# Two roundings of squares moved later in ScalarE's order, in a fused cross-attention and feed-forward kernel

## The chip, the cores and the metric

The kernel runs on one core of one Trainium2 chip. The metric is the device time of one execution in microseconds (us). A core has five engines that run beside each other and meet at semaphores: TensorE (PE; its weight loads are listed apart as PEld), VectorE (DVE), ScalarE (ACT), GpSimd (POOL) and SyncE (SP), which issues the DMAs. Each engine works through its own instructions in the order in which the program lists them: an instruction that waits holds all that stand behind it on its engine.

## What is computed

```python
x = x + tanh(g_xattn) * xattn(layernorm(x), ctx)
x = x + tanh(g_ffn)   * ffn(layernorm(x))
# xattn: 16 heads of 32, softmax(Q K^T / sqrt(32)) V, then Wo; 154 context rows per batch
# ffn, with x_prev the row before:
xr = mu_r * x + (1 - mu_r) * x_prev
xk = mu_k * x + (1 - mu_k) * x_prev
out = sigmoid(xr @ W_r.T) * (square(relu(xk @ W_k.T)) @ W_v.T)
```

x is (4, 2048, 512) in float32, all weights are 512 x 512. The product with W_v needs the squares of all 512 columns of relu(k).

## The kernel before, in words

The 8192 rows are cut into 16 blocks of 512 tokens. Every float32 product is made of three products of parts: each operand is split into an upper part (HI, rounded by a copy on ScalarE) and a lower part (LO, the source minus the upper part, a subtraction on VectorE or GpSimd), and TensorE multiplies HI by HI, HI by LO and LO by HI. A product of 512 x 512 by 128 columns is thus 12 matmuls of 128x128 by 512 columns.

Each engine has a function `step(i, ffn, pre)`, which is called for block 0 with ffn False, for blocks 1 to 14 in a hardware loop with both True, and for block 15 with pre False. A step works on the attention of block i and, with ffn True, on the feed-forward part of block i - 1; with pre True also on the first norm and the queries of block i + 1. The order of the work in a step is written out by hand, per engine.

The attention of a block goes through four groups g of four heads. For a group, TensorE makes scores of four banks (`head_scores`, L1187) and of the 26 tail rows of the context (`tail_scores`, L1202), ScalarE takes two exponentials of each of the five banks (`exps(i, g, n)`, n = 0 to 4, L656: one into `pq` as float16 at L662, one in place at L663), VectorE subtracts (`p_low`, L890), and TensorE multiplies with the values (`values`, L1209, waits for all five `p_low` of the group). VectorE then divides by the sum of the exponentials (`attend(i, g)`, L894: transposed, reciprocal, transposed, multiplied, each waiting for the one before, into `attn32`), ScalarE rounds that (`attn_high`, L675) and GpSimd makes its lower part (`attn_low`, L488).

The squares of relu(k) come in four chunks c of 128 columns, through two buffers in turn, `k2[c % 2]`, which are two slots of `place`:

- relu: chunks 0 and 1 on ScalarE (`k_relu`, L651), 2 and 3 on VectorE (`k_relu`, L911). VectorE's waits at L913 until the lower part of chunk c - 2, which reads the same buffer, is made: `k2_lo >= i*C + c - 1`.
- square: `k2_square(i, c)` on GpSimd (L480), in place.
- upper part: `k2_high(i, c)` on ScalarE (L647, recorded as L568, a helper), into `buf1`.
- lower part: `k2_low(i, c)` on GpSimd (L484), which waits for the upper part.

GpSimd's order (`k2_parts`, L500) is square 0, low 0, square 1, low 1, square 2, low 2, square 3, low 3. Behind it in the step stand the small operations of two norms (L449) and `attn_low(i, 0)`.

On VectorE, `k_relu(i-1, 2)` stands ahead of `p_low(i, 0, 0)` and `k_relu(i-1, 3)` behind `p_low(i, 0, 4)`; then come the moments of two tiles of the next block (`moments1`, L853), then `attend(i, 0)`, then `p_low(i, 1, 0)`.

TensorE's order from the first group's scores to the second group's values is: `head_scores(i, 0)`, `ffn_k(i-1, (3,))`, `tail_scores(i, 0)`, `ffn_r(i-1, 0)`, `values(i, 0)`, `head_scores(i, 1)`, `ffn_r(i-1, 1)` (waits for relu 3), `tail_scores(i, 1)` (waits for `p_low(i, 1, 0)`, L1203), `ffn_v(i-1, 0)` (waits for all four lower parts of the squares, L1301), `values(i, 1)`. These products are recorded at L1114, a helper; ffn_r's read WrT and ffn_v's read WvT.

Of the kernel before, what the change touches and what calls it, by code (L numbers as in the profile page):

```python
# [17 lines left out]
def flamingo_block(nc, x, ctx_columns, g_xattn, g_ffn, Wq, Wk, Wv, Wo, W_r, W_k, W_v, mu_r, mu_k, out):  # L18
# [30 lines left out]
    with ExitStack() as ctx:  # L49
# [516 lines left out]
        def _(act):  # L566
            def high(dst, src, done):
                nc.scalar.activation(dst, src, ACT.Copy).then_inc(done, 1)  # L568
# [19 lines left out]
            def kv_high(u):  # L588
                item, kind, n = KV[u]
                act.wait_ge(kv_done, u + 1)  # L590
                if item == 1 and kind == "k" and n >= 2:
                    act.wait_ge(later_stored[n - 2], 48)
                elif (item, kind, n) == (1, "v", 0):
                    act.wait_ge(v_stored, 32)
                    act.wait_ge(v_loaded, 16 * V_LOADS)
                if (item, kind, n) == (0, "v", 0):
                    act.wait_ge(mask_ready, 1)
                    nc.scalar.activation(kv_place(u, HI), kv_product(u), ACT.Copy, scale=mask[:, :]).then_inc(kv_hi, 1)
                else:
                    high(kv_place(u, HI), kv_product(u), kv_hi)  # L600
# [5 lines left out]
            def norm1(i, t):  # L606
                act.wait_ge(norm_ready[0], i * TT + t + 1)
                nc.scalar.activation(xa[:, t, :], xa[:, t, :], ACT.Identity, bias=nb[:, 0, t:t + 1],
                                     scale=rstd[:, 0, t:t + 1]).then_inc(xn1_ready, 1)
# [6 lines left out]
            def norm2(i, t, pre):  # L616
                if t >= 2:
                    act.wait_ge(x2_done, i * TT + t - 1)
                elif pre:
                    act.wait_ge(xT_done, (i + 1) * TT + t + 1)  # L620
                act.wait_ge(norm_ready[1], i * (TT - 1) + t + 1)
                nc.scalar.activation(xn2[t % 2], x1[:, t, :], ACT.Identity, bias=nb[:, 1, t:t + 1],  # L622
                                     scale=rstd[:, 1, t:t + 1]).then_inc(xn2_ready, 1)

            def xT_high(i, t):
                act.wait_ge(xT_done, i * TT + t + 1)
                later(act, q_done, i * G)
                high(xnT[:, HI, :, P * t:P * t + P], xT_bank[t][:, :].rearrange("p (c n) -> p c n", c=C), xT_hi)
# [14 lines left out]
            def q_split(i, g, loop):  # L643
                q_high(i, g, loop)
                q_copy(i, g, loop)

            def k2_high(i, c):  # L647
                act.wait_ge(k2_ready, i * C + c + 1)
                high(buf1[:, HI, c, :], k2[c % 2], k2_hi)

            def k_relu(i, c):  # L651
                act.wait_ge(k_done, i * C + c + 1)
                later(act, k2_lo, i * C)
                nc.scalar.activation(k2[c], K_BANK[c][:, :], ACT.Relu).then_inc(relu_ready[0], 1)  # L654

            def exps(i, g, n):  # L656

                m = 5 * g + n
                bank = score_bank[m]
                act.wait_ge(scores_done, i * SCORE_UNITS + m + 1)  # L660
                later(act, av_done, i * G + g)
                nc.scalar.activation(pq[:, n, HI, :], bank[:, :], ACT.Exp, scale=SCALE).then_inc(p_hi, 1)  # L662
                nc.scalar.activation(bank[:, :], bank[:, :], ACT.Exp, scale=SCALE).then_inc(p_full, 1)  # L663

            def tanh_r(i, t, bank=R_BANK):
                act.wait_ge(r_done, i * TT + t + 1)
                if t >= 2:
                    act.wait_ge(out_ready, i * TT + t - 1)
                else:

                    act.wait_ge(k2_lo, i * C + 1)
                    act.wait_ge(xr_mixed, i * C + 1)
                nc.scalar.activation(th[t % 2], bank[t][:, :], ACT.Tanh, scale=0.5).then_inc(th_ready, 1)

            def attn_high(i, g):  # L675
                act.wait_ge(attn32_ready, i * G + g + 1)
                high(buf3[:, HI, g, :], attn32, attn_hi)

            def x2_copy(i, t):
                act.wait_ge(x2_done, i * TT + t + 1)  # L680
                later(act, r_done, i * TT)
                dst, src = x2[:, :, 1 + P * t:1 + P * t + P], x2_bank[t][:, :].rearrange("p (c n) -> p c n", c=C)
                if t < TT - 1:
                    nc.scalar.activation(dst, src, ACT.Copy).then_inc(x2_ready, 1)
                else:

                    nc.scalar.activation(dst[:, 0:2, :], src[:, 0:2, :], ACT.Copy).then_inc(x2_half, 1)
                    nc.scalar.activation(dst[:, 2:4, :], src[:, 2:4, :], ACT.Copy).then_inc(x2_ready, 1)
# [5 lines left out]
            def xr_high(i, c):  # L694
                mix_high(i, buf2, c, xr_bank, xr_mixed, xr_hi)

            def xk_high(i, c):
                mix_high(i, buf3, c, xk_bank, xk_mixed, xk_hi)

            def mT_copy(i):  # L700
                act.wait_ge(mT_done, i + 1)
                high(mT[:, :], mT_bank[:, :], mT_ready)
# [20 lines left out]
            def fill_group(g):  # L723
                late = (units(5), units(6), ())[g]
                for u in late[:2]:
                    weight_high(u)
                kv_high(FIRST_LATER + 2 * g + 1)
                for u in late[2:]:
                    weight_high(u)

            def step(i, ffn, pre):
                if ffn:
                    k_relu(i - 1, 0)
                    k_relu(i - 1, 1)
                    xr_high(i - 1, 0)
                mT_copy(i)
                if ffn:
                    k2_high(i - 1, 0)
                    xr_high(i - 1, 1)
                    xr_high(i - 1, 2)  # L740
                exps(i, 0, 0)
                exps(i, 0, 1)
                if ffn:
                    xr_high(i - 1, 3)
                    k2_high(i - 1, 1)
                exps(i, 0, 2)
                exps(i, 0, 3)
                if not ffn:
                    kv_high(FIRST_LATER)
                exps(i, 0, 4)  # L750
                if ffn:
                    k2_high(i - 1, 2)
                    tanh_r(i - 1, 0)
                    k2_high(i - 1, 3)
                else:
                    fill_group(0)
                for g in range(1, G):
                    exps(i, g, 0)
                    exps(i, g, 1)
                    attn_high(i, g - 1)  # L760
                    if not ffn and g == 3:
                        kv_high(KV_UNITS - 1)
                    if pre and g == 3:
                        xT_high(i + 1, 0)
                    exps(i, g, 2)
                    exps(i, g, 3)
                    if not ffn and g < 3:
                        kv_high(FIRST_LATER + 2 * g)
                    exps(i, g, 4)
                    if ffn and (pre or g < G - 1):  # L770
                        tanh_r(i - 1, g)
                    elif not ffn and g < 3:
                        fill_group(g)
                    if pre:
                        for t in ((0, 1), (2, 3), ())[g - 1]:
                            norm1(i + 1, t)
                if pre:
                    for t in range(1, TT):
                        xT_high(i + 1, t)
                attn_high(i, G - 1)  # L780
                if not pre:
                    tanh_r(i - 1, TT - 1)
                if pre:
                    for g in range(G - 1):
                        q_split(i + 1, g, True)
                if not ffn:
                    for n in range(7):
                        act.wait_ge(later_stored[n], LATER_STORES[n])
                for t in range(TT):
                    if t < TT - 1:  # L790
                        norm2(i, t, pre)
                    x2_copy(i, t)
                if pre:
                    q_split(i + 1, 3, True)
                for c in range(C):
                    xk_high(i, c)

            step(0, False, True)
            with act.Fori(1, BLOCKS - 1) as i:
                step(i, True, True)  # L800
# [671 lines left out]
```

## Time and profile before

| | |
|---|---|
| time, median of 3 runs | 1404.73 us (1402.91 to 1406.04) |
| the profiled execution: its own time | 1408.19 us |
| the profiled execution: its span, first to last instruction | 1406.4 us |
| TensorE matmul busy | 1358.7 us, 97% of the span |
| VectorE busy | 1037.4 us, 74% |
| ScalarE busy | 777.4 us, 55% |
| GpSimd busy | 590.5 us, 42% |
| mean granted TensorE clock | 0.99 of full |

The loop blocks repeat to within a few hundredths of a microsecond, one every 83.0 us. In the timelines each line is a start in us from the span's start, a duration in us, the engine, the line of the kernel, the operation, what it writes and reads, how many were merged, and in brackets how long the engine had been idle before it and for whom. On ScalarE and VectorE the next instruction may start before the last one has fully ended, so steps in time are taken from start to start.

### The profile page before, as it was taken

The numbers are of one execution on the slowest core, as the hardware profiler recorded it, in microseconds if no ns is written. First come the engines' busy times: TensorE is split into PE (matmuls) and PEld (weight loads), VectorE is DVE, ScalarE is ACT, GpSimd is POOL, SyncE is SP. The second block draws the span as 40 slices with busy tenths as digits, with TensorE's granted clock in tenths as the row PEclk, the third lists the DMA queues.
The fourth block names the chain that finished last, engine by engine and source line by source line (L and its number), as shares of the span: only waits on it lengthen the run. The fifth ranks groups of instructions, "written<-read, shape, count | busy, mean of one in ns | idle before, by whom it ended". The sixth has DMA issues, their size and how long they took to land.

```text
span 1406.4 us, 27977 instructions
## 1 busy us (share of the span) xinstructions
PE 1358.7 (97%) x9436; PEld 992.8 (71%) x9436; DVE 1037.4 (74%) x1928; ACT 777.4 (55%) x1440; POOL 590.5 (42%) x786
## 2 busy tenths in 40 slices
PE   6889999999999999999999999999999999999988
PEld 5656676777767677676777767677776767777667
DVE  5867768687777868778786877868677686877652
ACT  5653746556374655737466473746637465573632
POOL 4333545343453534435353443525344352534333
PEclk8999999999999999999999999999999999999989
DMA  9421011212021121101212111121201112120101
GB/s 298 138 74 46 31 46 60 67 52 58 24 74 45 52 74 52 50 24 67 59 52 74 52 42 33 60 67 52 73 33 51 44 60 67 52 65 18 44 17 44
DMA packets 99179, 84.07 MB, mean 60 GB/s; under 512 B 49488, under 2 KB 64336, under 8 KB 99152
## 3 DMA queue, kind: packets, MB, share of 16 engines
q1 hardware_dynamic: 99152, 83.72, 19.5%
q8 instruction: 15, 0.25, 0.1%
q14 instruction: 12, 0.10, 0.0%
HBM read 57.75 MB, written 20.71 MB: 56 GB/s over the span
## 4 chain that ended last, share of the span: by engine, by line
PE 80%; DVE 8%; ACT 8%; issue 2%; DMA 1%; POOL 1%; SPq 0%; ACTq 0%; DVEq 0%
PE g_bank L1114 45%; PE g_bank L1274 7%; PE o_bank L1221 6%; PE s_bank L1195 4%; PE d_bank L1227 4%; ACT s_bank L663 3%; ACT pq L662 3%; PE s_bank L1171 3%; PE s_bank L1205 2%; DVE buf L815 2%; PE s_bank L1114 2%; PE d_bank L1120 2%; DVE o_bank L955 2%; PE o_bank L1120 1%; DVE d_bank L955 1%
## 5 line engine op out<-in xcount | busy, mean ns | idle before, releaser
L892 DVE TENSOR_TENSOR pq<-s_bank,pq 128x512 f16<-128x512 f32 x320 | 220.4, 689 | 68.9 <-ACT s_bank L663 68.4
L888 DVE TENSOR_REDUCE mm<-s_bank 128x3 f32<-128x462 f32 (+1 forms) x384 | 198.9, 578 | 96.1 <-PE s_bank L1171 96.1
L662 ACT ACTIVATE pq<-s_bank 128x512 f16<-128x512 f32 x320 | 192.2, 601 | 89.3 <-PE s_bank L1199 89.3
L1274 PE MATMUL g_bank<-buf,WkT 128*128 128x512 f32 x744 | 197.0, 412 | 8.6 <-DVE buf L815 6.9
L1114 PE MATMUL g_bank<-xnT,WqT 128*128 128x512 f32 x756 | 196.3, 406 | 0.0
L663 ACT ACTIVATE s_bank<-s_bank 128x512 f32<-128x512 f32 x320 | 194.6, 608 | 0.0
L1114 PE MATMUL g_bank<-WoT,buf 128*128 128x512 f32 x768 | 193.3, 401 | 0.0
L1114 PE MATMUL g_bank<-WrT,buf 128*128 128x512 f32 x744 | 184.2, 397 | 0.0
L490 POOL TENSOR_TENSOR buf<-place,buf 128x512 fp32r<-128x512 f32 x64 | 82.6, 1291 | 235.0 <-ACT buf L568 235.0
L1114 PE MATMUL g_bank<-WvT,buf 128*128 128x512 f32 x708 | 174.4, 395 | 0.0
L1274 PEld LDWEIGHTS g_bank<-buf,WkT 128*128 128x128 f32 x744 | 136.9, 192 | 51.7 <-DVE buf L815 13.8
L1114 PEld LDWEIGHTS g_bank<-WrT,buf 128*128 128x128 f32 x744 | 137.9, 188 | 40.2 <-issue 11.3
L1114 PEld LDWEIGHTS g_bank<-WoT,buf 128*128 128x128 f32 x768 | 140.8, 188 | 32.6
L1114 PEld LDWEIGHTS g_bank<-xnT,WqT 128*128 128x128 f32 x756 | 137.5, 190 | 35.6 <-DVE xnT L876 5.9
L1114 PEld LDWEIGHTS g_bank<-WvT,buf 128*128 128x128 f32 x708 | 130.7, 188 | 32.8 <-issue 5.8
L478 POOL TENSOR_TENSOR buf<-xa,buf 128x512 fp32r<-128x512 f32 x64 | 82.3, 1285 | 153.8 <-DVE d_bank L955 81.9
L568 ACT ACTIVATE buf<-place 128x512 fp32r<-128x512 f32 x128 | 81.0, 633 | 109.3 <-DVE place L909 74.8
L486 POOL TENSOR_TENSOR buf<-place,buf 128x512 fp32r<-128x512 f32 x64 | 83.2, 1300 | 94.0 <-ACT buf L568 94.0
L498 POOL TENSOR_TENSOR x<-place,x 128x512 f32<-128x512 f32 x48 | 61.7, 1286 | 123.1 <-DVE place L919 123.1
L622 ACT ACTIVATE xa<-x,nb,rstd 128x512 f32<-128x512 f32 x48 | 39.0, 813 | 105.2 <-POOL nb L460 104.9
L903 DVE STREAM_TRANSPOSE place<-d_bank 128x512 f32<-128x512 f32 x64 | 45.4, 709 | 62.2 <-PE d_bank L1227 59.1
L482 POOL TENSOR_TENSOR place<-place 128x512 f32<-128x512 f32 x64 | 78.2, 1221 | 25.6 <-ACT place L654 25.6
(145 smaller groups left out, 2087.9 us busy)
## 6 DMA issues: line engine op xcount, KB each, us to landing
xa<-in_x SPq DMA_DIRECT2D x64, 256.0 KB, 3.2
x<-in_x SPq DMA_DIRECT2D x64, 256.0 KB, 2.7
out<-x SPq DMA_DIRECT2D x48, 256.0 KB, 2.0
place<-x SPq DMA_DIRECT2D x16, 256.0 KB, 2.4
out<-place SPq DMA_DIRECT2D x16, 256.0 KB, 2.0
k_all<-k_scratch SPq DMA_DIRECT2D x15, 256.0 KB, 2.9
k_low<-k_scratch SPq DMA_DIRECT2D x15, 256.0 KB, 2.9
v_main<-v_scratch SPq DMA_DIRECT2D x15, 256.0 KB, 2.8
```

The costliest lines, as they stand in the source:

```text
L478: nc.gpsimd.tensor_tensor(buf4[:, LO, g, :], q32[g], buf4[:, HI, g, :].bitcast(F32), ALU.subtract).then_inc(q_lo, 1)
L482: nc.gpsimd.tensor_tensor(k2[c % 2], k2[c % 2], k2[c % 2], ALU.mult).then_inc(k2_ready, 1)
L486: nc.gpsimd.tensor_tensor(buf1[:, LO, c, :], k2[c % 2], buf1[:, HI, c, :].bitcast(F32), ALU.subtract).then_inc(k2_lo, 1)
L490: nc.gpsimd.tensor_tensor(buf3[:, LO, g, :], attn32, buf3[:, HI, g, :].bitcast(F32), ALU.subtract).then_inc(attn_lo, 1)
L568: nc.scalar.activation(dst, src, ACT.Copy).then_inc(done, 1)
L662: nc.scalar.activation(pq[:, n, HI, :], bank[:, :], ACT.Exp, scale=SCALE).then_inc(p_hi, 1)
L663: nc.scalar.activation(bank[:, :], bank[:, :], ACT.Exp, scale=SCALE).then_inc(p_full, 1)
L888: nc.vector.reduce_max(maxima, scores, AX.X).then_inc(reduced, 1)
L892: nc.vector.tensor_tensor(pq[:, n, LO, :], score_bank[5 * g + n][:, :], pq[:, n, HI, :], ALU.subtract).then_inc(p_lo, 1)
L1114: ins = nc.tensor.matmul(dst, stationary(s, c), moving(m, c), start=(c, n) == (0, 0), stop=(c, n) == (chunks - 1, len(PRODUCTS) - 1))
L1221: nc.tensor.matmul(o_bank[rows(j), :], v, pq[:, 4 if n else j, q, :], start=(n, k) == (0, 0), stop=(n, k) == (1, 2))
L1274: ins = nc.tensor.matmul(bank[c][:, :], WkT2[:, s, e, cols(c)], buf3[:, m, e, :], start=(e, n) == (0, 0), stop=(e, n) == (C - 1, len(PRODU ...
```

## The change

In ScalarE's step, with ffn True, three roundings of squares move. `k2_high(i-1, 1)` moves from ahead of `exps(i, 0, 2)` to behind `exps(i, 0, 4)`. `k2_high(i-1, 2)` moves from ahead of `tanh_r(i-1, 0)` to behind it. `k2_high(i-1, 3)` moves from behind `tanh_r(i-1, 0)` into the second group, behind `attn_high(i, 0)` and ahead of `exps(i, 1, 2)`. Nothing is added or removed, and no other engine's order changes.

```diff
@@ -742,22 +742,23 @@
                 exps(i, 0, 1)
                 if ffn:
                     xr_high(i - 1, 3)
-                    k2_high(i - 1, 1)
                 exps(i, 0, 2)
                 exps(i, 0, 3)
                 if not ffn:
                     kv_high(FIRST_LATER)
                 exps(i, 0, 4)
                 if ffn:
+                    k2_high(i - 1, 1)
+                    tanh_r(i - 1, 0)
                     k2_high(i - 1, 2)
-                    tanh_r(i - 1, 0)
-                    k2_high(i - 1, 3)
                 else:
                     fill_group(0)
                 for g in range(1, G):
                     exps(i, g, 0)
                     exps(i, g, 1)
                     attn_high(i, g - 1)
+                    if ffn and g == 1:
+                        k2_high(i - 1, 3)
                     if not ffn and g == 3:
                         kv_high(KV_UNITS - 1)
                     if pre and g == 3:
```

## Rows read from the trace of the kernel before

**Rows 1.** The page's first part: busy time, share of the span, instructions.
```profile
PE 1358.7 (97%) x9436; PEld 992.8 (71%) x9436; DVE 1037.4 (74%) x1928; ACT 777.4 (55%) x1440; POOL 590.5 (42%) x786
```
**Rows 2.** Waits of TensorE: in total us, times, longest.
```profile
PE o_bank L1221 <- DVE pq L892: 12.3, 20, 2.5
```
**Rows 3.** Timeline of TensorE, first and second head group of a loop block.
```profile
643.43 2.91 PE L1114 MATMUL g_bank<-WrT,buf 128*128 128x512 f32 x12
646.83 0.83 PE L1221 MATMUL o_bank<-pq,v_main 128*32 128x512 f16 x12 [0.49 <-DVE pq L892]
...
649.10 0.74 PE L1195 MATMUL s_bank<-buf,k_all 32*128 32x512 f32 x8
...
650.24 3.02 PE L1114 MATMUL g_bank<-WrT,buf 128*128 128x512 f32 x12
653.09 0.86 PE L1205 MATMUL s_bank<-buf,k_tail 128*128 128x512 f32 x3
...
654.01 2.90 PE L1114 MATMUL g_bank<-WvT,buf 128*128 128x512 f32 x12
656.85 0.83 PE L1221 MATMUL o_bank<-pq,v_main 128*32 128x512 f16 x12
```
**Rows 4.** Timeline of ScalarE, the same stretch.
```profile
642.25 0.64 ACT L568 ACTIVATE buf<-place 128x512 fp32r<-128x512 f32 x1
...
645.23 0.63 ACT L663 ACTIVATE s_bank<-s_bank 128x512 f32<-128x512 f32 x1
...
646.37 0.60 ACT L673 ACTIVATE place<-g_bank 128x512 f32<-128x512 f32 x1
648.79 0.63 ACT L568 ACTIVATE buf<-place 128x512 fp32r<-128x512 f32 x1 [1.82 <-POOL place L482]
...
651.90 0.60 ACT L663 ACTIVATE s_bank<-s_bank 128x512 f32<-128x512 f32 x1
652.41 0.63 ACT L568 ACTIVATE buf<-place 128x512 fp32r<-128x512 f32 x1
652.93 0.59 ACT L662 ACTIVATE pq<-s_bank 128x512 f16<-128x512 f32 x1
```
**Rows 5.** Timeline of VectorE, the same stretch.
```profile
645.89 0.69 DVE L892 TENSOR_TENSOR pq<-s_bank,pq 128x512 f16<-128x512 f32 x1 [0.31 <-ACT s_bank L663]
646.50 0.68 DVE L914 TENSOR_SCALAR place<-g_bank 128x512 f32<-128x512 f32 x1
...
649.22 0.72 DVE L903 STREAM_TRANSPOSE place<-d_bank 128x512 f32<-128x512 f32 x1 [0.18 <-PE d_bank L1227]
...
651.01 0.69 DVE L909 TENSOR_TENSOR place<-o_bank,place 128x512 f32<-128x512 f32 x1
651.61 0.68 DVE L892 TENSOR_TENSOR pq<-s_bank,pq 128x512 f16<-128x512 f32 x1
```
**Rows 6.** Timeline of GpSimd, the same stretch.
```profile
646.48 1.28 POOL L486 TENSOR_TENSOR buf<-place,buf 128x512 fp32r<-128x512 f32 x1 [1.23 <-ACT buf L568]
647.72 1.04 POOL L482 TENSOR_TENSOR place<-place 128x512 f32<-128x512 f32 x1
649.50 1.29 POOL L486 TENSOR_TENSOR buf<-place,buf 128x512 fp32r<-128x512 f32 x1 [0.74 <-ACT buf L568]
```
**Rows 7.** Timeline, a restart of TensorE after a wait: VectorE, TensorE, its weight loads.
```profile
631.03 0.69 DVE L815 TENSOR_TENSOR buf<-o_bank,buf 128x512 fp32r<-128x512 f32 x1
...
631.77 3.06 PE L1274 MATMUL g_bank<-buf,WkT 128*128 128x512 f32 x12 [0.16 <-DVE buf L815]
634.76 0.34 PE L1171 MATMUL s_bank<-k_all,buf 32*128 32x154 f32 x4
...
631.77 2.62 PEld L1274 LDWEIGHTS g_bank<-buf,WkT 128*128 128x128 f32 x12 [0.59 <-DVE buf L815]
```
**Rows 8.** Timeline of TensorE, two waits close together at the end of block 0's step.
```profile
127.56 0.57 PE L1171 MATMUL s_bank<-k_all,buf 32*128 32x154 f32 x12 [1.33 <-ACT buf L568]
129.62 7.40 PE L1274 MATMUL g_bank<-buf,WkT 128*128 128x512 f32 x24 [1.49 <-DVE buf L815]
```
**Rows 9.** Busy time by stretch there: stretch, its length, engines, granted clock, DMA.
```profile
129.60:132.00 2.40, 2.38 (x6) 1.90 (x7) 2.36 (x4) 0.91 (x3) 0.26 (x1) 0.53 0.00 0
```

## The prediction

> **What bounds the kernel now.** I read the engines' busy shares first: TensorE is busy for 97% of the span, VectorE for 74%, ScalarE for 55% and GpSimd for 42% [rows 1]. So an edit on ScalarE can matter only through a wait of TensorE: one that it removes, or one that it makes. Next I read TensorE's waits. One of them belongs to the stretch that is edited: the product with the values waits for VectorE's subtraction, 12.3 us over 20 times [rows 2]. Then I read four engines' timelines side by side over one loop block. TensorE waits 0.49 us ahead of the first group's values at 646.83 and has no gap behind it up to the second group's values at 656.85 [rows 3]. The reader should see two things there. The subtraction that ends this wait runs from 645.89 to 646.58 and follows the last exponential of the group, which starts at 645.23 [rows 4, 5]. And the squares' lower parts are early now: the last one ends at 649.50 + 1.29 = 650.79, and its reader, the first product with WvT, starts at 654.01 [rows 3, 6], so that path has 3.2 us to spare.
>
> **What the first move gives.** A rounding of a square takes ScalarE 0.52 us from its start to the next start (652.41 to 652.93; the rounding there is of the attention, of the same shape) [rows 4]. The one at 642.25 stands ahead of three pairs of exponentials. Behind its removal they all start 0.52 us earlier, the last at 644.71; its scores don't hold it, since the tail's matmuls are issued ahead of the product that starts at 643.43 [rows 3] and end within some 0.2 us of that. The last subtraction then ends at 646.06. TensorE would be free by itself at 643.43 + 2.84 = 646.27, taking 2.84 us for twelve matmuls, from 654.01 to 656.85 [rows 3]. So the wait goes and the values start about 0.53 us earlier, at 646.3. This is the gain: 0.5 us a block, if nothing later takes it.
>
> **What the same move costs on VectorE.** The rounding of chunk 1 now starts at 645.23 and ends at 645.87. GpSimd starts a lower part 0.08 us behind its rounding (648.79 + 0.63 = 649.42 to 649.50 [rows 4, 6]), so at 645.95, and needs 1.29: until 647.24. VectorE's relu of chunk 3 writes the same buffer and waits for that (L913). It started at 646.50 [rows 5] and now starts at about 647.3, so 0.8 us later. Behind it in VectorE's queue are the moments of two tiles, the first group's `attend`, and the first subtraction of the second group, for which TensorE's tail scores wait. From the relu to `attend` it is 2.72 us with 0.18 idle in it [rows 5]; since neighbours on VectorE overlap by about 0.08 (645.89 + 0.69 against 646.50 [rows 5]), I take 2.45 as the least distance. `attend` thus starts at 649.75 in place of 649.22, although TensorE now delivers half a microsecond earlier. Its last operation starts 1.79 us later (651.01 less 649.22), at 651.54, and ends at 652.23. The subtraction behind it starts 2.39 us behind `attend`'s start [rows 5], at 652.14, and ends at 652.82. TensorE would want to start the tail scores at 653.09 - 0.53 = 652.56, and starts at 652.87. With the restart (next but one paragraph) they are done at 653.94, where they were done at 654.01. So on this path alone the gain is all but used up already.
>
> **What the third move costs.** The rounding of chunk 3 stands behind `attn_high` of the first group now, which waits for `attend`: it can't start before 652.23 + 0.04. It started at 652.41 and was held by ScalarE's own order then [rows 4]; now `attend` holds it, and it starts at about 652.28. The rounding of chunk 3 follows at 652.80 and ends at 653.43. GpSimd's lower part follows at 653.51 and ends at 654.80. Its square isn't late for this: lower part 1 until 647.24, square 2 (1.04 [rows 6]) until 648.25, its rounding until 648.92, lower part 2 until 650.25, square 3 until 651.3. TensorE restarts at 654.85, 0.05 us behind what it waited for (631.03 + 0.69 to 631.77 [rows 7]). The product with WvT wants to start at 653.94 and so waits 0.9 us, a wait that isn't in the trace of before. The lower part that had 3.2 us to spare has none.
>
> **The restart.** Twelve matmuls after a wait took 2.99 us up to the next start, 631.77 to 634.76 [rows 7], against 2.84 without one [rows 3]: 0.15 more. The first weight load of that restart and the first matmul both stand at 631.77 [rows 7]: the loads had not been made during the wait. The Trainium skill, in "TensorE: Matmul & The Clock Gate", "Step-by-step: what each phase is for", says that TensorE loads weights ahead of matmuls that are still in flight. If it did so here across the wait, the 0.15 would fall away and the sum would be 1417.5; the row speaks against that for this kind of wait.
>
> **The sum.** The second group's values start at 654.85 + 2.99 = 657.84 in place of 656.85: 1.0 us later per block. Their own subtractions don't hold them longer: the last exponential of the group keeps its place from before but for the two 0.52 us that go and come, and its subtraction ends at about 657.1. Behind the values I found no gap of TensorE in the two groups that follow, so nothing there gives the time back; the shift passes into the next block, and the blocks come one every 84.0 us in place of 83.0. GpSimd's queue behind the lower part (two norms, about 1 us each, then the lower part of the attention) moves by 4 us and ends near 658.3; its readers are VectorE's `attend` of the second group, at 660.5 then, and ScalarE's norms, which have over 2 us until the third group's scores. The second move (chunk 2 behind `tanh_r`) costs nothing: `tanh_r` starts at 646.37, when its product is done, and chunk 2's square is done only at 648.25. No DMA is moved. The change works in 15 steps (blocks 1 to 15). Block 15 has no moments on VectorE, so it loses a little less; I don't take that off. 15 x 1.0 = 15.0 us. On the profiled execution it is 1408.2 + 15.0 = 1423.2 (its span 1406.4 to 1421.4); that execution stands 3.5 us above the median of the runs shown, and from the median I forecast **1419.7 us**.
>
> **Bounds of the unknown terms.** The trace of before shows no wait of TensorE for GpSimd. From below: if VectorE's lateness didn't reach `attn_high`, ScalarE's order alone would put it 0.53 us earlier than now (651.88), and the WvT product would start at 651.88 + 0.52 + 0.63 + 0.08 + 1.29 + 0.05 = 654.45; with the restart this is 0.6 us a block, 9 us in all, 1413.7. From above: if `attend` keeps its whole 2.72 us behind the relu, 0.27 us more a block, 1.27 x 15 = 19 us, 1423.8. I take a value between, nearer the row-by-row sum, for the reason given there. A further 0.1 us for lags leaves 1412 to 1426.
>
> **The rivals.** (a) *The gain stays* (faster). The wait of 0.49 us goes and the last lower part still comes in time. The point from which this decides is 653.5: a lower part that ends by then holds nobody. It would give 15 x 0.5 = 7.5 us less, 1397. For it speaks that GpSimd is busy only for 42% [rows 1] and had 3.2 us to spare; against it, that the four steps from `attn_high` on (0.52, 0.63, 0.08, 1.29) put it at 654.4 at the earliest, and 654.8 by my chain. (b) *Gain and loss cancel* (no change). VectorE's lateness sends the tail scores back to their old time, but the lower part of chunk 3 holds nobody. That is 653.94 against 654.01, or 1404. It needs the same 0.9 us error in the chain behind `attn_high`. (c) *The clock falls as well* (slower by more). Two waits of 1.33 and 1.49 us close together [rows 8] were followed by a granted clock of 0.53 [rows 9], its lower level of 1.2 GHz being half, and 24 matmuls took 7.40 us where they take 2 x 2.84 = 5.68: 1.7 us. I forecast two waits of about 0.3 and 0.9 us, not half as long together. If it happened in each block: 15 x 2.7 = 41 us, 1445. That the edit doesn't do what it says can be left out: the order is written out by hand and followed literally.
>
> **How the numbers follow.** Chance of the forecast with its bounds (1412 to 1426): 0.88. Of (a) 0.04, of (b) 0.04, of (c) 0.04. The range 1412 to 1426 leaves out 0.12. A measurement of this kernel can tell about 0.2%, 2.8 us, from no change: faster 0.04, same 0.04, slower 0.92.
>
> **What would show it right or wrong.** In the changed kernel's trace: no wait ahead of the first group's values; VectorE idle for some 1.3 us ahead of the relu at L914, released by GpSimd's L486; ScalarE's `attn_high` of the first group released by VectorE's L909; a new wait of TensorE of about 0.9 us ahead of the first WvT product, released by L486; a small one of 0.3 us ahead of the second group's tail scores; 84.0 us from block to block; the granted clock still 1.00. The prediction is wrong if L486's last run ends ahead of 653.5 on the scale used here, or if a later slack takes up the shift.

## The result, and the profile after

The changed kernel takes 1420.56 us, median of 4 runs (1420.11 to 1421.07), against 1403.93 (1402.91 to 1406.04, 4 runs) for the kernel before: a ratio of 1.0117, with an interval of 1.0099 to 1.0134. It is slower, by 16.6 us from median to median; the forecast was 1419.7, slower by 15.0. The profiled execution took 1420.30 us, its span is 1418.6 us.

The page's first part for the changed kernel, where [rows 1] stand for before: TensorE is busy for 3.2 us more in a longer span, and the busy times of the other engines are within 3 us of what they were.

```profile
PE 1361.9 (96%) x9436; PEld 988.8 (70%) x9436; DVE 1034.8 (73%) x1928; ACT 779.0 (55%) x1440; POOL 589.0 (42%) x786
```

The timeline of TensorE in a loop block, from the first group's last product with WrT to the second group's values. It answers [rows 3]; this block lies 4.34 us later than that one (647.77 here, 643.43 there), so 4.34 is to be taken off for a comparison. Code lines behind the edit are numbered one higher here (L1222 is L1221 of before).

```profile
647.77 2.91 PE L1115 MATMUL g_bank<-WrT,buf 128*128 128x512 f32 x12
650.65 0.83 PE L1222 MATMUL o_bank<-pq,v_main 128*32 128x512 f16 x12
...
654.06 3.03 PE L1115 MATMUL g_bank<-WrT,buf 128*128 128x512 f32 x12
657.25 0.97 PE L1206 MATMUL s_bank<-buf,k_tail 128*128 128x512 f32 x3 [0.15 <-DVE pq L893]
...
659.27 2.98 PE L1115 MATMUL g_bank<-WvT,buf 128*128 128x512 f32 x12 [0.83 <-POOL buf L486]
662.19 0.83 PE L1222 MATMUL o_bank<-pq,v_main 128*32 128x512 f16 x12
...
741.22 0.96 PE L1206 MATMUL s_bank<-buf,k_tail 128*128 128x512 f32 x3 [0.18 <-DVE pq L893]
```

The reader sees the wait ahead of the values at 650.65 gone, a short one of 0.15 us ahead of the tail scores, and a new one of 0.83 us ahead of the first WvT product, whose releaser is GpSimd's lower part, L486. The last line is the same tail scores one block later: 741.22 - 657.25 = 83.97 us from block to block, against 83.0.

The three engines behind that wait, the same stretch, as [rows 4], [rows 5] and [rows 6] show it for before: VectorE, ScalarE, GpSimd.

```profile
651.69 0.69 DVE L915 TENSOR_SCALAR place<-g_bank 128x512 f32<-128x512 f32 x1 [1.28 <-POOL buf L486]
...
654.15 0.68 DVE L904 STREAM_TRANSPOSE place<-d_bank 128x512 f32<-128x512 f32 x1
...
655.90 0.69 DVE L910 TENSOR_TENSOR place<-o_bank,place 128x512 f32<-128x512 f32 x1
...
656.63 1.15 ACT L568 ACTIVATE buf<-place 128x512 fp32r<-128x512 f32 x2 [0.32 <-DVE place L910]
...
650.30 1.28 POOL L486 TENSOR_TENSOR buf<-place,buf 128x512 fp32r<-128x512 f32 x1 [4.77 <-ACT buf L568]
...
657.86 1.27 POOL L486 TENSOR_TENSOR buf<-place,buf 128x512 fp32r<-128x512 f32 x1 [2.25 <-ACT buf L568]
```

This is the chain read backwards: the lower part at 657.86 waited 2.25 us for the second of the two roundings that are merged at 656.63; the first of those is `attn_high`, released by VectorE's L910, the end of `attend`; `attend` came late because VectorE had stood 1.28 us ahead of its relu at 651.69, for the lower part of chunk 1 at 650.30. (The lines stand by engine, as in [rows 4] to [rows 6], not in one order of time.)

The granted clock of TensorE stayed at its upper level around the new waits: it is the 1.00 in the row of the stretch from 657 to 661.

```profile
657.00:661.00 4.00, 3.02 (x13) 2.13 (x13) 2.39 (x5) 4.00 (x9) 2.85 (x6) 1.00 0.00 0
```

### The profile page after: what moved, and what is told of

It is laid out like the page before. It is cut to its first block, busy times and chain, and to the rows that moved or that the text cites. A ratio compares the mean times of both kernels' runs of the same rounds, so it can differ in the third digit from the quotient of the medians.

```text
span 1418.6 us, 27977 instructions
## 1 busy us (share of the span) xinstructions
PE 1361.9 (96%) x9436; PEld 988.8 (70%) x9436; DVE 1034.8 (73%) x1928; ACT 779.0 (55%) x1440; POOL 589.0 (42%) x786
## 3 DMA queue, kind: packets, MB, share of 16 engines
q1 hardware_dynamic: 99152, 83.72, 19.5%
## 4 chain that ended last, share of the span: by engine, by line
PE 64%; issue 18%; POOL 11%; ACT 3%; DVE 2%; DMA 1%; SPq 0%; POOLq 0%; ACTq 0%; DVEq 0%
PE g_bank L1115 42%; PE o_bank L1222 5%; POOL place L482 5%; POOL buf L486 4%; PE d_bank L1228 3%; PE s_bank L1172 2%; PE s_bank L1196 2%; PE d_bank L1121 2%; PE s_bank L1206 2%; PE s_bank L1115 2%; PE s_bank L1121 1%; POOL place L498 1%; PE g_bank L1275 1%; PE o_bank L1121 1%; ACT buf L568 1%
## 5 line engine op out<-in xcount | busy, mean ns | idle before, releaser
L893 DVE TENSOR_TENSOR pq<-s_bank,pq 128x512 f16<-128x512 f32 x320 | 217.4, 687 | 62.3 <-ACT s_bank L663 60.6
L486 POOL TENSOR_TENSOR buf<-place,buf 128x512 fp32r<-128x512 f32 x64 | 83.0, 1296 | 154.0 <-ACT buf L568 154.0
```

Of the source, the lines that this page charges most:

```text
L486: nc.gpsimd.tensor_tensor(buf1[:, LO, c, :], k2[c % 2], buf1[:, HI, c, :].bitcast(F32), ALU.subtract).then_inc(k2_lo, 1)
L893: nc.vector.tensor_tensor(pq[:, n, LO, :], score_bank[5 * g + n][:, :], pq[:, n, HI, :], ALU.subtract).then_inc(p_lo, 1)
```

## The experiments

All times are device times against the kernel before, run in turn on the same chip. The table sets the block time in the trace (from one start to the same start a block later) beside the measured difference. Each series of runs had its own runs of the kernel before, so each row names the median that it is compared with.

| kernel | us per block | 15 x (block - 82.97) | ratio measured (interval) | median, before |
|---|---|---|---|---|
| changed kernel | 83.97 | +15.0 | 1.0117 (1.0099 to 1.0134) | 1420.56, 1403.93 |
| third move alone | 84.05 | +16.2 | 1.0118 (1.0101 to 1.0135) | 1422.54, 1406.21 |
| first moves without the third | 84.33 | +20.4 | 1.0137 (1.0120 to 1.0154) | 1425.74, 1406.21 |
| change, rounding 3 ahead of attn_high | 83.05 | +1.2 | 1.0011 (1.0001 to 1.0021) | 1407.28, 1406.21 |
| change, first moments ahead of relu 3 | 83.55 | +8.7 | 1.0045 (1.0028 to 1.0062) | 1413.82, 1406.21 |
| change, both swaps | 83.06 | +1.4 | 1.0008 (0.9999 to 1.0017) | 1407.04, 1406.38 |
| roundings 0 and 1 early | 82.97 | 0 | 0.9996 (0.9987 to 1.0005) | 1405.69, 1406.38 |
| the same, GpSimd's order kept | 83.40 | +6.5 | 1.0042 (1.0029 to 1.0055) | 1412.69, 1406.38 |
| roundings early, lower parts 0, 1 behind the mixes | 82.45 | -7.8 | 0.9935 (0.9922 to 0.9949) | 1397.00, 1405.03 |
| roundings early, lower part 1 behind the mixes | 82.63 | -5.1 | 0.9962 (0.9948 to 0.9977) | 1400.53, 1405.03 |

### Taking the change apart

**The third move alone.**

```diff
                 if ffn:
                     k2_high(i - 1, 2)
                     tanh_r(i - 1, 0)
-                    k2_high(i - 1, 3)
...
                     attn_high(i, g - 1)
+                    if ffn and g == 1:
+                        k2_high(i - 1, 3)
```

> Only the rounding of chunk 3 moves (behind attn_high of the first group); chunks 1 and 2 stay as in the kernel before. My theory: the chain attn_high, rounding 3, lower part 3 holds the WvT product even when nothing on VectorE is late. On the scale of the kernel before: attn_high 652.41, rounding 652.93 to 653.56, lower part 653.64 to 654.93, product restarts at 655.0 with 0.15 for the restart, against 654.01: 1.1 us a block, and the wait of 0.49 us ahead of the first group's values stays. 15 blocks: 17 us slower than before, about 1421, as slow as the changed kernel. Rival (the loss comes from VectorE's late relu of chunk 3, which is early here): within 3 us of the kernel before.

Measured: 1422.54 us, 16.3 us more than before. TensorE keeps its old wait of 0.50 us and gets the new one of 0.86. ScalarE waits for nobody ahead of `attn_high`, the first of the two roundings merged in the last line:

```profile
651.21 0.83 PE L1222 MATMUL o_bank<-pq,v_main 128*32 128x512 f16 x12 [0.50 <-DVE pq L893]
659.42 2.98 PE L1115 MATMUL g_bank<-WvT,buf 128*128 128x512 f32 x12 [0.86 <-POOL buf L486]
...
656.78 1.14 ACT L568 ACTIVATE buf<-place 128x512 fp32r<-128x512 f32 x2
```

So the place of the third rounding is enough for the whole loss, with VectorE in time. VectorE's late relu isn't needed for it: relu 3 starts at 646.51 on the scale of the kernel before (4.37 taken off), where it started at 646.50, and the block takes as long as with the whole change.

**The first moves without the third.**

```diff
                     xr_high(i - 1, 3)
-                    k2_high(i - 1, 1)
...
                 if ffn:
-                    k2_high(i - 1, 2)
+                    k2_high(i - 1, 1)
                     tanh_r(i - 1, 0)
+                    k2_high(i - 1, 2)
                     k2_high(i - 1, 3)
```

> The rounding of chunk 1 moves behind the first group's exponentials, chunk 2 behind tanh, and chunk 3 stays in the first group, behind chunk 2 and ahead of the second group's exponentials. My theory: chunk 3's square is only ready at 651.3 on the scale of the kernel before (relu 3 at 647.3, lower part 2 until 650.25, square 1.04), so ScalarE stands there until 651.3 and the second group's exponentials start 1.4 us later than before; the second group's last subtraction ends at about 658.2 in place of 656.7. About 1.4 us a block, 21 us, 1425: worse than the changed kernel, so the third move made up for a part of what the first one costs. Rival (the third move is the whole loss and the first alone keeps its gain of 0.5 us a block): 1397.

Measured: 1425.74 us, 19.5 us more. ScalarE stands for chunk 3's square ahead of the second group's exponentials, and TensorE in turn ahead of that group's tail scores and its values:

```profile
656.11 0.63 ACT L568 ACTIVATE buf<-place 128x512 fp32r<-128x512 f32 x1 [1.30 <-POOL place L482]
659.14 0.63 ACT L568 ACTIVATE buf<-place 128x512 fp32r<-128x512 f32 x1 [2.40 <-POOL place L482]
659.68 0.58 ACT L662 ACTIVATE pq<-s_bank 128x512 f16<-128x512 f32 x1
...
661.52 0.96 PE L1205 MATMUL s_bank<-buf,k_tail 128*128 128x512 f32 x3 [0.96 <-DVE pq L892]
...
666.04 0.83 PE L1221 MATMUL o_bank<-pq,v_main 128*32 128x512 f16 x12 [0.60 <-DVE pq L892]
```

The third move thus repairs a part (84.33 to 83.97) of what the first one causes: once the rounding of chunk 1 is late, chunk 3's square is late too, and the rounding of chunk 3 has no good place.

### Taking its two waits away

The edits of the next three kernels are shown against the changed kernel.

**Rounding 3 ahead of `attn_high`.**

```diff
                     exps(i, g, 1)
-                    attn_high(i, g - 1)
                     if ffn and g == 1:
                         k2_high(i - 1, 3)
+                    attn_high(i, g - 1)
```

> The changed kernel with one swap: the rounding of chunk 3 stands ahead of attn_high of the first group, not behind it, so it doesn't wait for VectorE's attend. My theory: rounding at 651.9 to 652.5, lower part 652.6 to 653.9, which is about when TensorE reaches the WvT product after the late tail scores (653.94). The wait of 0.83 us goes, the one of 0.15 us ahead of the tail scores stays: 0 to 0.1 us a block, 1404 to 1406, within 2 us of the kernel before. Rival (GpSimd itself is the bound, whatever the order on ScalarE): the wait stays above 0.5 us a block, 1415 or more.

Measured: 1407.28 us, ratio 1.0011. No wait for GpSimd is recorded any more, and that ahead of the tail scores is left:

```profile
644.15 0.83 PE L1222 MATMUL o_bank<-pq,v_main 128*32 128x512 f16 x12
...
650.74 0.96 PE L1206 MATMUL s_bank<-buf,k_tail 128*128 128x512 f32 x3 [0.18 <-DVE pq L893]
...
651.86 3.00 PE L1115 MATMUL g_bank<-WvT,buf 128*128 128x512 f32 x12
...
650.44 1.28 POOL L486 TENSOR_TENSOR buf<-place,buf 128x512 fp32r<-128x512 f32 x1 [1.33 <-ACT buf L568]
```

Swapping two neighbouring roundings on ScalarE, 0.52 us each, gives back 0.9 us a block: 0.52 for the place in the order and the rest because the rounding no longer waits for `attend`. The slack is used up, though: the lower part ends at 650.44 + 1.28 = 651.72, and the product starts 0.14 us behind it, as far behind as in the changed kernel (659.13 to 659.27), where it did wait.

**First moments ahead of relu 3 (VectorE).**

```diff
-                if ffn:
-                    k_relu(i - 1, 3)
...
                 if pre:
                     moments1(i + 1, 0)
+                if ffn:
+                    k_relu(i - 1, 3)
+                if pre:
                     moments1(i + 1, 1)
```

> The changed kernel with one swap on VectorE: the moments of the first tile stand ahead of the relu of chunk 3, so they fill the 1.28 us in which VectorE waited for the lower part of chunk 1. ScalarE's order is that of the change. My theory: attend starts 0.9 us earlier, attn_high is held by ScalarE's own order again (651.9 on the scale of the kernel before), lower part 3 ends at 654.4, and the WvT product restarts at 654.45: 0.6 us a block, 9 us, 1413. This is the lower bound of the prediction. Rival (VectorE's wait is the whole loss): the gain of 0.5 us a block stands, 1397; rival (VectorE's wait doesn't matter): 1420 as the change.

Measured: 1413.82 us, 7.6 us more than before, 83.55 us a block. VectorE waits 0.35 us in place of 1.28, and `attn_high` (the first rounding of the second line) follows ScalarE's own order. TensorE's wait for GpSimd stays and ends 0.4 us earlier in the block: at 654.53 on the scale of the kernel before (3.96 taken off), where the change has 654.93.

```profile
651.32 0.69 DVE L915 TENSOR_SCALAR place<-g_bank 128x512 f32<-128x512 f32 x1 [0.35 <-POOL buf L486]
...
655.85 1.14 ACT L568 ACTIVATE buf<-place 128x512 fp32r<-128x512 f32 x2
...
658.49 2.97 PE L1116 MATMUL g_bank<-WvT,buf 128*128 128x512 f32 x12 [0.86 <-POOL buf L486]
```

**Both swaps.** The two edits above together.

> The changed kernel with both swaps (rounding of chunk 3 ahead of attn_high, VectorE's first moments ahead of the relu of chunk 3). My theory: all is on time but the last lower part, which ends at 651.88 + 0.63 + 0.08 + 1.29 = 653.88 on the scale of the kernel before, while TensorE reaches the WvT product at 653.48 now; it waits 0.4 us and restarts with 0.15 more, so the second group's values start at 656.9 in place of 656.85. 0 to 0.1 us a block: 0 to 2 us slower than the kernel before. The gain of 0.5 us can't be kept while the rounding of chunk 1 stands behind the exponentials. Rival (the two swaps undo both losses, 0.6 and 0.4, so the gain of 0.5 stays): 7 us faster than the kernel before.

Measured: 1407.04 us, ratio 1.0008. The tail scores come in time, and the wait for the last lower part is back at 0.36 us:

```profile
656.93 2.98 PE L1116 MATMUL g_bank<-WvT,buf 128*128 128x512 f32 x12 [0.36 <-POOL buf L486]
```

So with the rounding of chunk 1 behind the exponentials none of the orders tried keeps the 0.5 us: what the first group's values win, the last lower part costs.

### Keeping the gain

**Roundings 0 and 1 early.** If ScalarE's path to the first group's last exponential is what holds the values, the rounding may leave it in the other direction, into idle time of ScalarE ahead of the exponentials.

```diff
 GpSimd, k2_parts
-                for c in range(C):
+                k2_square(i, 0)
+                k2_square(i, 1)
+                k2_low(i, 0)
+                k2_low(i, 1)
+                for c in (2, 3):
                     k2_square(i, c)
                     k2_low(i, c)
 ScalarE, step
                     xr_high(i - 1, 0)
+                    k2_high(i - 1, 0)
                 mT_copy(i)
                 if ffn:
-                    k2_high(i - 1, 0)
                     xr_high(i - 1, 1)
+                    k2_high(i - 1, 1)
                     xr_high(i - 1, 2)
...
                     xr_high(i - 1, 3)
-                    k2_high(i - 1, 1)
```

> The kernel before, with the roundings of chunks 0 and 1 moved the other way, into idle time of ScalarE: rounding 0 ahead of the copy of the maxima, where ScalarE was idle 1.22 us, rounding 1 between the roundings of xr 1 and xr 2, where it was idle 0.51 us ahead of the first exponential; for that GpSimd makes square 1 ahead of lower part 0. My theory: three pairs of exponentials start 0.52 us earlier as in the change, but no lower part and no relu is later than before. The wait of 0.49 us ahead of the first group's values goes and nothing takes its place: 82.5 us a block in place of 83.0, 7 us faster than the kernel before, ratio 0.995. Rival (what bounds the values is not ScalarE's order, or square 1 comes too late and holds the exponentials): no faster than the kernel before.

Measured: 1405.69 us, ratio 0.9996. The expected 7 us didn't come, though the wait ahead of the values did go. VectorE's mixes of xr (one scalar_tensor_tensor each) all took 0.75 to 0.76 us in the kernel before. Here the last three of a block took 0.92, 1.65 and 1.08, the first of them begun beside GpSimd's squares and the other two beside its subtractions, and these took 3.44 us for two in place of 2.6. VectorE, GpSimd, and then TensorE's new wait:

```profile
634.77 0.92 DVE L969 SCALAR_TENSOR_TENSOR d_bank<-place,mu,x 128x512 f32<-128x512 f32 x1
635.74 1.65 DVE L969 SCALAR_TENSOR_TENSOR o_bank<-place,mu,x 128x512 f32<-128x512 f32 x1
...
638.01 1.08 DVE L969 SCALAR_TENSOR_TENSOR d_bank<-place,mu,x 128x512 f32<-128x512 f32 x1
...
632.78 2.35 POOL L482 TENSOR_TENSOR place<-place 128x512 f32<-128x512 f32 x2 [1.21 <-ACT place L658]
635.09 3.44 POOL L486 TENSOR_TENSOR buf<-place,buf 128x512 fp32r<-128x512 f32 x2
...
640.93 0.96 PE L1209 MATMUL s_bank<-buf,k_tail 128*128 128x512 f32 x3 [0.34 <-DVE pq L896]
```

**The same with GpSimd's order kept**, and rounding 1 behind the rounding of xr 2:

```diff
 ScalarE, step
                     xr_high(i - 1, 0)
+                    k2_high(i - 1, 0)
                 mT_copy(i)
                 if ffn:
-                    k2_high(i - 1, 0)
                     xr_high(i - 1, 1)
                     xr_high(i - 1, 2)
+                    k2_high(i - 1, 1)
...
                     xr_high(i - 1, 3)
-                    k2_high(i - 1, 1)
```

> As e6, but GpSimd keeps its order (square 0, lower 0, square 1, lower 1), and rounding 1 stands behind the rounding of xr 2, next ahead of the first exponential. Square 1 then ends at 639.3 to 639.8 on the scale of the kernel before (1.04 us alone, 1.52 as in the trace of before beside VectorE's mixes), and the first exponential, which could start at 639.77, starts at 639.8 to 640.3: between the whole gain of 7 us and none. I expect half of it, 3 us faster than the kernel before. If it is no slower than e6, the order on GpSimd didn't matter.

Measured: 1412.69 us, 6.3 us slower where I expected 3 faster: a miss. Lower part 0 took 1.80 us, the mix that began beside it 1.48, the square behind it 1.49. ScalarE stood 1.06 us for that mix and 0.29 for that square ahead of the first exponential, and TensorE's wait ahead of the first group's values grew from 0.49 to 0.75 us. VectorE, ScalarE, GpSimd, TensorE:

```profile
640.77 1.48 DVE L965 SCALAR_TENSOR_TENSOR o_bank<-place,mu,x 128x512 f32<-128x512 f32 x1 [0.22 <-ACT mT L568]
...
642.29 0.60 ACT L568 ACTIVATE buf<-o_bank 128x512 fp32r<-128x512 f32 x1 [1.06 <-DVE o_bank L965]
643.18 0.63 ACT L568 ACTIVATE buf<-place 128x512 fp32r<-128x512 f32 x1 [0.29 <-POOL place L482]
643.72 0.58 ACT L662 ACTIVATE pq<-s_bank 128x512 f16<-128x512 f32 x1
...
639.90 1.80 POOL L486 TENSOR_TENSOR buf<-place,buf 128x512 fp32r<-128x512 f32 x1 [0.74 <-ACT buf L568]
641.66 1.49 POOL L482 TENSOR_TENSOR place<-place 128x512 f32<-128x512 f32 x1
...
650.25 0.83 PE L1221 MATMUL o_bank<-pq,v_main 128*32 128x512 f16 x12 [0.75 <-DVE pq L892]
```

**Lower parts behind the mixes.** Two waits more in the version with roundings 0 and 1 early:

```diff
                 k2_square(i, 1)
+                pool.wait_ge(xr_mixed, i * C + 3)
                 k2_low(i, 0)
+                pool.wait_ge(xr_mixed, i * C + 4)
                 k2_low(i, 1)
```

> e6 with two waits more on GpSimd: lower part 0 waits for VectorE's mix of xr 2, lower part 1 for the mix of xr 3, so that GpSimd's subtractions no longer run beside the mixes. In e6 these mixes took 0.92, 1.65 and 1.08 us in place of 0.76, VectorE came 1.3 us late to the first subtraction of the group, and the gain of 0.5 us a block was lost at the tail scores. My theory (the two engines slow each other): the mixes take 0.76 again, the wait ahead of the tail scores goes, and the block takes 82.5 us: 7 us faster than the kernel before, ratio 0.995. Rival (the mixes are slow for another reason, or the new waits only shift the trouble to the relu of chunk 2): as e6, no gain.

Measured: 1397.00 us, ratio 0.9935 (0.9922 to 0.9949): faster than the kernel before, and so than the changed one. The mix that no GpSimd instruction runs beside is back at 0.76. The one that begins beside the squares is still at 0.92, and the last one, which begins while lower part 0 runs, at 1.38; so the mixes aren't all at 0.76 as I expected. VectorE is early enough all the same. VectorE, GpSimd, TensorE:

```profile
632.62 0.92 DVE L971 SCALAR_TENSOR_TENSOR d_bank<-place,mu,x 128x512 f32<-128x512 f32 x1
633.60 0.76 DVE L971 SCALAR_TENSOR_TENSOR o_bank<-place,mu,x 128x512 f32<-128x512 f32 x1
...
634.99 1.38 DVE L971 SCALAR_TENSOR_TENSOR d_bank<-place,mu,x 128x512 f32<-128x512 f32 x1
...
630.65 2.34 POOL L482 TENSOR_TENSOR place<-place 128x512 f32<-128x512 f32 x2 [1.22 <-ACT place L660]
634.52 1.29 POOL L486 TENSOR_TENSOR buf<-place,buf 128x512 fp32r<-128x512 f32 x1 [1.54 <-DVE o_bank L971]
636.53 1.30 POOL L486 TENSOR_TENSOR buf<-place,buf 128x512 fp32r<-128x512 f32 x1 [0.71 <-DVE d_bank L971]
...
642.11 0.83 PE L1227 MATMUL o_bank<-pq,v_main 128*32 128x512 f16 x12
...
724.56 0.83 PE L1227 MATMUL o_bank<-pq,v_main 128*32 128x512 f16 x12
```

**Only lower part 1 behind the mixes.** As the last one, without the first of its two waits.

> e6 with one wait more on GpSimd: only lower part 1 waits for the mix of xr 3; lower part 0 still runs beside the mix of xr 1. My theory: the mix beside lower part 0 still takes about 1.0 to 1.6 us, the others 0.76, so VectorE comes 0.3 to 0.8 us late in place of 1.3; TensorE's wait ahead of the tail scores (0.34 in e6) shrinks or goes. Between e6 and e8, nearer to e8: 4 to 7 us faster than the kernel before. Rival (as for e8): as e6.

Measured: 1400.53 us, ratio 0.9962. The mix that begins beside lower part 0 takes 1.64 us, the next one 0.76:

```profile
633.18 1.64 DVE L970 SCALAR_TENSOR_TENSOR o_bank<-place,mu,x 128x512 f32<-128x512 f32 x1
...
635.45 0.76 DVE L970 SCALAR_TENSOR_TENSOR d_bank<-place,mu,x 128x512 f32<-128x512 f32 x1
```

Of the 0.52 us a block that both waits gain over the early roundings without them (82.97 to 82.45), that of lower part 1 alone brings 0.34 (82.97 to 82.63); adding that of lower part 0 brings the other 0.18.

The slow mix follows the GpSimd instruction from place to place in four kernels, so that the two belong together is shown. The times also tell how: the one that begins second is held up until about the end of the first. All nine slow mixes of a block in these four kernels (0.82 to 1.65 us) end 0.55 to 0.56 us behind the GpSimd instruction that was running when they began, whether that is a square or a subtraction. With both lower parts behind the mixes, for example, the squares end at 630.65 + 2.34 = 632.99 and the mix of 0.92 at 633.54; lower part 0 ends at 635.81 and the mix of 1.38 at 636.37. A mix that begins first keeps its 0.76, and GpSimd's instruction is late instead: the lower part of 1.80 us ends 1.15 behind the mix of 0.76 that was running when it began (639.79 to 640.55), and the square of 1.49 ends 0.90 behind the mix of 1.48. So a slow mix's time tells how much of GpSimd's instruction was left, and not which kind it was. What in the chip they share isn't shown by a run. The Trainium skill, in "GPSIMD Engine Reference", "Key points", says that GpSimd shares its interfaces to SBUF with VectorE and that the two contend where a VectorE instruction has two SBUF inputs. The mixes do have two (`diff` and `x2`). VectorE's subtractions with one operand in PSUM kept their 0.67 to 0.69 us in these traces. The trace agrees.

## Why the prediction was right, point by point

It was right in direction, in size and in mechanism, with two small errors that cancel by luck (the restart, below). With 4.34 us taken off, the steps of the prediction stand beside the trace as follows.

| step | forecast | trace |
|---|---|---|
| wait ahead of the first group's values | gone | gone |
| VectorE idle ahead of relu 3 | 1.3 | 1.28 |
| relu 3 starts | 647.3 | 647.35 |
| `attend` starts | 649.75 | 649.81 |
| tail scores start | 652.87 | 652.91 |
| wait recorded ahead of them | 0.3 | 0.15 |
| `attn_high` starts | 652.28 | 652.29 |
| lower part 3 | 653.51 to 654.80 | 653.52 to 654.79 |
| WvT product starts | 654.85 | 654.93 |
| wait recorded ahead of it | 0.9 | 0.83 |
| second group's values start | 657.84 | 657.85 |
| block to block | 84.0 | 83.97 |

The recorded waits are shorter than the delays, because they are counted from the modelled end of the matmuls before: the WrT product ends at 654.06 + 3.03 = 657.09 by the record, and the tail scores of the kernel before start 0.17 us ahead of such an end (650.24 + 3.02 against 653.09). The start times are what the sum needs, and they agree.

**The gain.** It was there (0.5 us a block) and was taken back within 7 us, as forecast. **VectorE's part.** From the relu to `attend` the trace has 2.46 us, where the prediction chose 2.45 and not 2.72; this is where the bounds were widest. The swap of the moments confirms the lower bound: 83.55 us a block, 0.58 more than before, where the prediction had 0.6. **The third move.** The swap with `attn_high` took the loss away, and the third move alone made all of it, so its place is the cause. No run has the second move (chunk 2 behind `tanh_r`) by itself; in the changed trace `tanh_r` starts at 646.38 on the scale of before and ScalarE then waits 1.30 us for chunk 2's square, which fits a cost of nothing. This also bears on how the prediction splits the loss: it has VectorE's lateness as a part of the chain, and in the whole change that is worth 0.4 us a block (83.97 against 83.55). With the third move alone VectorE is in time, but ScalarE reaches `attn_high` later by its own order (656.78 - 4.37 = 652.41, against 652.29 in the change), and the loss is the same.

**The restart.** I priced it at 0.05 us of lag and 0.15 for twelve matmuls; measured are 0.14 (659.13 to 659.27) and 0.08 (2.92 to the next start against 2.84). The sums are nearly the same, 0.20 and 0.22, but that is luck: the lag was read from a matmul that waits for VectorE, and behind GpSimd it is 0.09 us longer, while the twelve matmuls lose 0.07 less. The weight loads of the WvT product did not begin during the wait: the first stands at 659.24, 0.03 ahead of the first matmul. So no load was made ahead across this wait, as [rows 7] had it.

**The sum.** 15 x 1.0 = 15.0 is what the block times give. From the first feed-forward product of block 0's step to that of the last step it is 1366.54 - 129.62 = 1236.92 us before and 1379.70 - 127.99 = 1251.71 here, 14.8 more over the same 15 steps. The last of them, block 15, loses a little less, as the prediction said: its wait ahead of the WvT product is 0.80 us. The medians are 16.6 apart, with an interval of 14 to 19 us (1.0099 to 1.0134 of 1404), so they agree with it; what the other 1.6 us are isn't shown. The spans of the two profiled executions are only 12.2 apart. Of what is missing there, 1.6 us lie ahead of the first block's feed-forward products (129.62 in [rows 8], 127.99 here), before the first step that the change touches. Another 1.0 us lies in the same 24 matmuls after the same wait of 2.78 us near the end: 8.39 us before and 7.38 here, with a granted clock of 0.50 over the first 2.5 us in the one and 0.76 in the other. Nothing links the second to the change either, but that is argued, not shown. Both are reasons to sum blocks and not spans.

**The rivals.** (a) and (b) needed the last lower part by 653.5; it came at 654.79. (c) the clock stayed at 1.00 through the two waits.

## What to carry to other kernels

On an engine that works in order, moving an instruction later to clear a path moves everything that follows from it as well: follow the product of the moved instruction to its last reader on every engine, and count the slack there, before counting the gain. A step that is off the path may be better moved ahead, into a gap in which its engine waits anyway. When a GpSimd instruction is moved, look at which VectorE instructions with two SBUF operands it will meet, and which of the two begins first, because the second ends late by what is left of the first.

## What the runs showed that I had not expected

VectorE's mix (one scalar_tensor_tensor over 128x512 with two operands in SBUF) took 0.76 us alone or when it began first, and up to 1.65 when it began while a GpSimd instruction ran; GpSimd's subtraction took up to 1.8 us in place of 1.29 when it began second. The trace of before held a hint of it on one side only: a GpSimd square of 1.52 us beside a mix, where others took 1.04, with the mix unchanged. It fits: that mix (639.54 to 640.30) began ahead of the square (639.67), and the square ended 0.89 us behind it. A small order of waits, two on GpSimd, was worth 8 us of 1405 because of this, and it made the difference between no gain and the fastest version of this study.
